# Audio tower: variance of a pair in two steps, a new order of all steps, and filling products behind the last round

## The chip, the cores and the metric

The kernel runs on one core of a Trainium2 chip. The metric is the device time of one execution in microseconds; lower is better. A core has five engines that run their own queues in order and meet at semaphores: PE (TensorE, matrix products), DVE (VectorE), ACT (ScalarE), POOL (GpSimd) and SP (SyncE, which issues DMAs).

## What is computed

The input is 64 records of 4000 samples. A tower of seven convolutions without padding follows (128 channels; taps and strides 10/5, four times 3/2, twice 2/2), each with a layer norm over the channels and an exact GELU. It leaves 12 positions for each record, 768 tokens of 128 channels. Then come a layer norm, a projection to 192, a Nyström attention with 64 landmarks and a mixture of eight experts with two chosen, beside a shared expert. The change touches the tower alone:

```python
for w, g, b, s in zip(conv_ws, ln_gs, ln_bs, strides):
    h = _conv1d(h, w, s)
    h = jnp.swapaxes(h, -2, -1)
    h = _fp32_layernorm(h, g, b)
    h = jnp.swapaxes(h, -2, -1)
    h = jax.nn.gelu(h, approximate=False)
```

## The kernel before, in words

The records go through the tower in four rounds of 16. A round has two slots (s = 0, 1) of eight records. Layers 0 to 3 are done round by round. Layers 4 to 6 take all 64 records at the end, and there a slot is half of them: slot 0 of layer 4 holds rounds 0 and 1, slot 1 rounds 2 and 3, and its pair p is the round 2s + p.

The order of all work is one list of steps, written out by hand. ROUND_ORDER is played once for each turn; a step is named what.layer.slot.p, a "+" in front means that it belongs to the next round, a "-" to the round before. LAST_ORDER is played once behind the turns. tower_plan makes the list and numbers the steps. Each engine walks the whole list and issues only what is its own share of each step, with waits for the numbers that it needs. So the list sets the order on every engine at once, and a step whose input is late holds up all that stands behind it on that engine. The steps:

- prep (parts 0 to 13) and phases: the windows of layer 0 for the next round, made by VectorE (and one copy on GpSimd for phases), written to DRAM and read back by SP's DMAs.
- first: layer 0 of one record, two bf16 matmuls (L476); ScalarE does the GELU (L562).
- half, conv: a pair of chunks of 400 columns. In layers 1 to 3 (PAIRED) half issues the middle tap (L499) and a product shared by both chunks (L502, ScalarE copies it); GpSimd forms a difference for conv (L457), which adds the outer taps (L508). VectorE writes the pair to SBUF (L682, in layers 4 to 6 L685) and ScalarE squares it (L579). In layers 4 to 6 half and conv are the two chunks (L522).
- var: the sum over channels of the squares of a pair, by matmuls in which the squares are the weights and one column of constants streams (L536): eight fp32 matmuls, which the profile shows as 16 instructions, since each fp32 matmul is two passes.
- norm: VectorE turns the variances of a whole slot into three bf16 parts of 1/sqrt(v + eps), 15 small operations (L694 to L706).
- rows: PE transposes them (L546), VectorE copies (L709). scale: PE spreads the row over the partitions (L553), VectorE multiplies one chunk (L715). gelu: ScalarE, on two chunks (L584).

PE has two banks for pairs and firsts, two for scales, and one for the shared product. There are two buffers of squares: ScalarE's square of a pair waits until the variance of the pair two before is done.

Before the change, half.4.0.0 stands behind all steps of layer 3 of the last round. Behind the tower, the attention's own products begin.

## Time and profile before

| what | value |
|---|---|
| median of 3 runs | 904.41 us (904.39 to 908.73) |
| the profiled execution | 903.9 us |
| its span | 901.8 us |
| PE busy | 752.5 us (83%) |
| VectorE busy | 640.3 us (71%) |
| ScalarE busy | 331.3 us (37%) |
| GpSimd busy | 313.0 us (35%) |
| mean granted clock of TensorE | 0.92 of full |

The span begins with the windows of round 0 (to about 55 us); the rounds fill 55 to about 447 us, the last layers end at 520.3 us, and attention and experts fill the rest. A busy PE isn't a PE at full speed: the granted clock tells at which of its two levels (1.2 or 2.4 GHz) it ran. Busy time is that of instructions, and an instruction lasts longer at the lower clock.

### The profile page before, as it was taken

To read this page: it belongs to the slowest core of one execution; us is meant where nothing else is said; L and a number is where in the kernel's file an instruction comes from. 1 tells how busy PE (TensorE), PEld (TensorE's weight loads), DVE (VectorE), ACT (ScalarE), POOL (GpSimd) and SP (SyncE) were. 2 spreads that over 40 slices of the span, in tenths; PEclk is the share of its full clock that TensorE was granted. 3 is DMA by queue.
4 is the path that set the end of the run, shared out by engine and by line. 5 is a ranking of instruction groups with operands and counts; after the bars stand their busy time and mean duration, and the time that the engine had idled before them with its cause. 6 is when DMAs were issued, how large, how long until landed. Compare 5 with 4: busy or idle time off the path is not lost. (4 is left out here: it accounts for less than half of the span.)

```text
span 901.8 us, 11857 instructions
## 1 busy us (share of the span) xinstructions
PE 752.5 (83%) x4259; PEld 574.4 (64%) x4259; DVE 640.3 (71%) x1447; ACT 331.3 (37%) x562; POOL 313.0 (35%) x365
## 2 busy tenths in 40 slices
PE   0039999999999999999787578788888888899987
PEld 0016565565655665665554477768788887899977
DVE  3946867887788966546646566998888888553387
ACT  0034456354544564454313215113333231346333
POOL 3003320412231312222100006475788787238301
PEclk9999978999799988998989589989999999989999
DMA  1360150006100330000000070000000000200000
GB/s 60 45 133 1 35 115 1 1 1 124 26 1 1 62 76 0 1 1 1 1 0 1 1 323 2 1 1 1 1 1 1 2 1 1 80 1 1 1 1 26
DMA packets 22564, 25.48 MB, mean 28 GB/s; under 512 B 17052, under 2 KB 21212, under 8 KB 21404
## 3 DMA queue, kind: packets, MB, share of 16 engines
q1 hardware_dynamic: 22508, 24.74, 11.2%
q8 instruction: 34, 0.56, 0.3%
q14 instruction: 22, 0.18, 0.1%
HBM read 21.05 MB, written 3.66 MB: 27 GB/s over the span
## 5 line engine op out<-in xcount | busy, mean ns | idle before, releaser
L457 POOL TENSOR_TENSOR diff<-h 128x400 f32<-128x400 f32 x112 | 97.6, 895 | 300.0 <-ACT h L562 135.1
L536 PEld LDWEIGHTS ps<-averager,sq 128*100 128x100 f32 (+2 forms) x1024 | 103.2, 176 | 16.7 <-ACT sq L579 8.1
L499 PE MATMUL ps<-h,w 128*128 128x400 f32 x224 | 109.9, 620 | 1.3 <-ACT h L584 0.5
L536 PE MATMUL ps<-averager,sq 128*100 128x1 f32 (+2 forms) x1024 | 101.1, 229 | 4.0 <-ACT sq L579 3.9
L682 DVE TENSOR_TENSOR h<-ps,shared 128x800 f32<-128x800 f32 x56 | 55.4, 989 | 57.2 <-PE ps L508 53.8
L579 ACT ACTIVATE sq<-h 128x800 f32<-128x800 f32 (+1 forms) x58 | 50.1, 864 | 118.7 <-DVE h L682 112.6
L508 PE MATMUL ps<-diff,w 128*128 128x400 f32 x224 | 91.1, 528 | 0.0
L1023 PE MATMUL pt<-for_pe,ident 128*128 128x156 f32 (+2 forms) x420 | 67.0, 318 | 23.4 <-DVE for_pe L1222 23.4
L562 ACT ACTIVATE h<-ps,lnp 128x800 f32<-128x800 f32 x64 | 63.5, 1014 | 47.5 <-PE ps L476 47.1
L1023 PEld LDWEIGHTS pt<-for_pe,ident 128*128 128x128 f32 x420 | 60.7, 196 | 28.5 <-DVE for_pe L1222 26.1
L476 PE MATMUL ps<-late,w_stack 90*128 90x400 bf16 x128 | 35.9, 383 | 49.1 <-DMA late<-windows_dram 45.0
L715 DVE TENSOR_TENSOR h<-h,ps 128x400 f32<-128x400 f32 (+1 forms) x116 | 61.0, 559 | 18.8 <-PE ps L553 17.7
L584 ACT ACTIVATE h<-h,lnp 128x800 f32<-128x800 f32 (+1 forms) x58 | 59.8, 1045 | 37.9 <-DVE h L715 36.7
L980 PE MATMUL pt<-ident 128*128 128x128 f32 x542 | 69.5, 289 | 0.0
L499 PEld LDWEIGHTS ps<-h,w 128*128 128x128 f32 x224 | 46.3, 219 | 35.3 <-issue 32.6
L980 PEld LDWEIGHTS pt<-ident 128*128 128x128 f32 x542 | 67.7, 205 | 0.6 <-issue 0.4
L508 PEld LDWEIGHTS ps<-diff,w 128*128 128x128 f32 x224 | 42.7, 198 | 28.9 <-issue 26.7
L476 PEld LDWEIGHTS ps<-late,w_stack 90*128 90x128 bf16 x128 | 12.5, 113 | 70.0 <-issue 57.8
L1242 DVE TENSOR_REDUCE e<-from_pool 128x54 f32<-128x702 f32 (+8 forms) x117 | 56.7, 550 | 0.3
L502 PE MATMUL ps<-h,w_sum 128*128 128x400 f32 x112 | 56.6, 590 | 0.0
L1023 PE MATMUL pt<-pool_for_pe,ident 128*128 128x132 f32 (+3 forms) x420 | 56.5, 292 | 0.0
L1088 POOL TENSOR_TENSOR from_pool<-e,c 128x702 f32<-128x702 f32 (+8 forms) x54 | 50.2, 973 | 18.0 <-DVE c L1324 18.0
(283 smaller groups left out, 1369.4 us busy)
## 6 DMA issues: line engine op xcount, KB each, us to landing
late<-windows_dram SPq DMA_DIRECT2D x24, 375.0 KB, 7.6
gate_w<-in_gate_w SPq DMA_DIRECT2D x1, 3456.0 KB, 14.0
up_w<-in_up_w SPq DMA_DIRECT2D x1, 3456.0 KB, 19.3
windows_dram<-parts SPq DMA_DIRECT2D x12, 250.0 KB, 5.4
acts<-in_down_w SPq DMA_DIRECT2D x1, 1728.0 KB, 8.1
w<-in_w SPq DMA_DIRECT2D x1, 1024.0 KB, 5.3
xs<-in_x SPq DMA_DIRECT2D x4, 252.5 KB, 4.7
out_tokens<-hidden SPq DMA_DIRECT2D x6, 96.0 KB, 1.6
```

What stands on the lines that cost most here:

```text
L457: pool.tensor_tensor(to[:, rows, :], here[:, rows, :], behind[:, rows, :], ALU.subtract).then_inc(diff_ready, 1)
L499: pe.matmul(out[:, c, :, :], w[:, L.first_tap + 1, :], plane(l, s, p, 1, slice(c, L.pos, 2)), start=True, stop=False)
L502: pe.matmul(shared_ps[:, 0:L.cols].rearrange("p (b t) -> p b t", t=L.pos // 2), w_sum[:, l - 1, :], plane(l, s, p, 0, slice(1, L.pos, 2)), ...
L508: mm = pe.matmul(out[:, c, :, :], w[:, L.first_tap + 2 * c, :], diffs(l, n["paired"] % RING, slice(c, L.pos, 2)), start=False, stop=True)
L536: mm = pe.matmul(var_ps[0:L.w, at:at + 1], sq[:, square_of[r, l, s, p] % 2, c, q * L.w:(q + 1) * L.w], averager[:, 0:1], start=True, stop= ...
L562: act.activation(h0[:, s, p, :, 0:POS0 // 2], ypair[b][:, :, 0:400], ACT.Gelu, scale=lnp[:, 0:1], bias=lnp[:, 1:2]).then_inc(y_taken, 1)
L584: act.activation(both, both, ACT.Gelu, scale=lnp[:, 2 * l:2 * l + 1], bias=lnp[:, 2 * l + 1:2 * l + 2]).then_inc(gelu_done, 1)
L682: nc.vector.tensor_tensor(to, src, both.unsqueeze(1).broadcast_to([P, 2, 2 * L.per_chunk, L.pos // 2]), ALU.add).then_inc(y_copied, 1)
L715: nc.vector.tensor_tensor(h, h, spread[n["scale"] % 2][:, 0:L.cols].rearrange("p (b t) -> p b t", t=h.shape[2]), ALU.mult).then_inc(scaled, 1)
L980: pe.matmul(to[:, 0:P], ident[:, :], ident[:, :], start=True, stop=True)
L1023: mm = pe.matmul(job.banks(n)[:, 0:wide], ident[:, :], sum_buffers[n][:, k * wide:(k + 1) * wide], start=(k == 0), stop=(k == job.terms - 1))
L1242: nc.vector.tensor_reduce(job.out(i), pooled_row(job, i), AX.X, ALU.add).then_inc(row_done, 1)
```

## The change

- A var step now covers one chunk of a pair instead of two (p counts chunks): eight passes instead of 16, each step with its own increment of var_done. ScalarE's square waits for both steps of the pair two before.
- ROUND_ORDER is new throughout. conv.1.0.0 of the next round now closes a turn. The four scales and two gelus of layer 3 stand further back in the next turn, behind steps of layers 1 and 2.
- There are turns only up to the last but one; LAST_ORDER now holds the whole last round, with layer 4's slot 0 between the steps of layer 3, and the last layers in a new order. The wait of layer 4's half and conv asks for the gelus of the one round that they read.
- A new step fill.0.0.n issues n products of 400 bf16 columns (ident16 by pick) into the bank of the shared product. Nothing reads them. LAST_ORDER has 13 such steps with 46 products.

```diff
--- before.py
+++ after.py
@@ -123,27 +123,41 @@
 
 
 ROUND_ORDER = """
-    conv.1.0.0 half.1.0.1 prep.0.0.4 first.0.0.5 -var.3.1.0 -norm.3.1.0 conv.1.0.1 var.1.0.0 -scale.3.0.0 prep.0.0.5 half.1.0.2
-    first.0.1.0 prep.0.0.6 conv.1.0.2 prep.0.0.7 prep.0.0.8 var.1.0.1 -rows.3.1.0 half.1.0.3 prep.0.0.9 first.0.1.3 conv.1.0.3
-    var.1.0.2 prep.0.0.10 first.0.1.6 first.0.1.2 -scale.3.0.1 -gelu.3.0.0 var.1.0.3 half.1.1.0 norm.1.0.0 conv.1.1.0 half.1.1.1
-    rows.1.0.0 -scale.3.1.1 -scale.3.1.0 -gelu.3.1.0 conv.1.1.1 scale.1.0.2 var.1.1.0 prep.0.0.11 first.0.1.5 first.0.1.4
-    scale.1.0.1 scale.1.0.0 gelu.1.0.0 var.1.1.1 first.0.1.7 half.1.1.2 prep.0.0.12 scale.1.0.3 gelu.1.0.1 conv.1.1.2 prep.0.0.13
-    half.1.1.3 conv.1.1.3 half.2.0.0 scale.1.0.7 scale.1.0.4 var.1.1.2 scale.1.0.6 gelu.1.0.3 scale.1.0.5 gelu.1.0.2 var.1.1.3
-    norm.1.1.0 conv.2.0.0 half.2.0.1 rows.1.1.0 conv.2.0.1 scale.1.1.0 scale.1.1.1 gelu.1.1.0 var.2.0.0 scale.1.1.3 scale.1.1.2
-    gelu.1.1.1 scale.1.1.5 scale.1.1.6 +first.0.0.3 +first.0.0.7 scale.1.1.4 gelu.1.1.2 scale.1.1.7 gelu.1.1.3 var.2.0.1 half.2.1.0
-    +phases.0.0.0 norm.2.0.0 +first.0.0.0 conv.2.1.0 rows.2.0.0 half.2.1.1 +prep.0.0.0 scale.2.0.0 +first.0.1.1 scale.2.0.1
-    gelu.2.0.0 conv.2.1.1 scale.2.0.3 scale.2.0.2 gelu.2.0.1 +first.0.0.6 +prep.0.0.1 var.2.1.0 var.2.1.1 half.3.0.0 norm.2.1.0
-    +first.0.0.4 conv.3.0.0 +first.0.0.1 rows.2.1.0 scale.2.1.3 scale.2.1.2 gelu.2.1.1 scale.2.1.1 scale.2.1.0 gelu.2.1.0
-    +prep.0.0.2 var.3.0.0 +first.0.0.2 half.3.1.0 norm.3.0.0 conv.3.1.0 +half.1.0.0 +prep.0.0.3 rows.3.0.0
+    -var.3.1.1 prep.0.0.3 -var.3.1.0 -norm.3.1.0 half.1.0.1 var.1.0.1 first.0.1.6 conv.1.0.1 prep.0.0.4 var.1.0.0 half.1.0.2
+    first.0.1.1 prep.0.0.5 prep.0.0.6 prep.0.0.7 conv.1.0.2 prep.0.0.8 prep.0.0.9 var.1.0.2 half.1.0.3 var.1.0.3 -rows.3.1.0
+    conv.1.0.3 var.1.0.4 var.1.0.5 first.0.1.4 first.0.1.5 var.1.0.6 var.1.0.7 prep.0.0.10 norm.1.0.0 first.0.1.3 half.1.1.0
+    -scale.3.1.0 first.0.1.7 conv.1.1.0 rows.1.0.0 prep.0.0.11 half.1.1.1 conv.1.1.1 prep.0.0.12 var.1.1.1 var.1.1.0 scale.1.0.3
+    half.1.1.2 scale.1.0.1 conv.1.1.2 var.1.1.3 var.1.1.2 half.1.1.3 prep.0.0.13 scale.1.0.2 gelu.1.0.1 var.1.1.4 scale.1.0.0
+    gelu.1.0.0 conv.1.1.3 var.1.1.5 scale.1.0.5 scale.1.0.7 half.2.0.0 scale.1.0.6 gelu.1.0.3 scale.1.0.4 gelu.1.0.2 conv.2.0.0
+    var.1.1.6 var.1.1.7 norm.1.1.0 half.2.0.1 conv.2.0.1 var.2.0.1 rows.1.1.0 -scale.3.0.1 scale.1.1.2 +first.0.0.4 +phases.0.0.0
+    +first.0.0.6 scale.1.1.5 var.2.0.3 scale.1.1.3 gelu.1.1.1 scale.1.1.1 var.2.0.0 scale.1.1.0 gelu.1.1.0 scale.1.1.4 gelu.1.1.2
+    +first.0.0.3 var.2.0.2 scale.1.1.7 scale.1.1.6 gelu.1.1.3 norm.2.0.0 half.2.1.0 conv.2.1.0 half.2.1.1 -scale.3.0.0 -gelu.3.0.0
+    rows.2.0.0 -scale.3.1.1 -gelu.3.1.0 conv.2.1.1 scale.2.0.0 scale.2.0.1 gelu.2.0.0 +first.0.0.1 var.2.1.0 scale.2.0.3 scale.2.0.2
+    gelu.2.0.1 var.2.1.3 +prep.0.0.0 var.2.1.1 var.2.1.2 +first.0.0.0 +first.0.1.0 +first.0.1.2 norm.2.1.0 half.3.0.0 rows.2.1.0
+    +first.0.0.2 scale.2.1.1 scale.2.1.0 gelu.2.1.0 conv.3.0.0 scale.2.1.2 scale.2.1.3 gelu.2.1.1 +prep.0.0.1 +first.0.0.5 var.3.0.0
+    var.3.0.1 norm.3.0.0 half.3.1.0 conv.3.1.0 +half.1.0.0 +prep.0.0.2 +first.0.0.7 rows.3.0.0 +conv.1.0.0
 """
 
 LAST_ORDER = """
-    half.4.0.0 conv.4.0.0 half.4.0.1 var.4.0.0 conv.4.0.1 half.4.1.0 var.4.0.1 norm.4.0.0 conv.4.1.0 half.4.1.1 rows.4.0.0
-    scale.4.0.0 scale.4.0.1 gelu.4.0.0 var.4.1.0 conv.4.1.1 scale.4.0.2 scale.4.0.3 gelu.4.0.1 half.5.0.0 var.4.1.1 norm.4.1.0
-    conv.5.0.0 rows.4.1.0 scale.4.1.0 scale.4.1.1 gelu.4.1.0 var.5.0.0 scale.4.1.2 scale.4.1.3 gelu.4.1.1 norm.5.0.0 half.5.1.0
-    rows.5.0.0 scale.5.0.0 scale.5.0.1 gelu.5.0.0 conv.5.1.0 half.6.0.0 var.5.1.0 norm.5.1.0 conv.6.0.0 rows.5.1.0 scale.5.1.0
-    scale.5.1.1 gelu.5.1.0 var.6.0.0 norm.6.0.0 half.6.1.0 rows.6.0.0 scale.6.0.0 scale.6.0.1 gelu.6.0.0 conv.6.1.0 var.6.1.0
-    norm.6.1.0 rows.6.1.0 scale.6.1.0 scale.6.1.1 gelu.6.1.0
+    -var.3.1.1 -var.3.1.0 -norm.3.1.0 half.1.0.1 var.1.0.1 first.0.1.6 conv.1.0.1 var.1.0.0 half.1.0.2 first.0.1.1 conv.1.0.2
+    var.1.0.2 half.1.0.3 var.1.0.3 -rows.3.1.0 conv.1.0.3 var.1.0.4 var.1.0.5 first.0.1.4 first.0.1.5 var.1.0.6 var.1.0.7 norm.1.0.0
+    first.0.1.3 half.1.1.0 -scale.3.1.0 first.0.1.7 conv.1.1.0 rows.1.0.0 half.1.1.1 conv.1.1.1 var.1.1.1 var.1.1.0 scale.1.0.3
+    half.1.1.2 scale.1.0.1 conv.1.1.2 var.1.1.3 var.1.1.2 half.1.1.3 scale.1.0.2 gelu.1.0.1 var.1.1.4 scale.1.0.0 gelu.1.0.0
+    conv.1.1.3 var.1.1.5 scale.1.0.5 scale.1.0.7 half.2.0.0 scale.1.0.6 gelu.1.0.3 scale.1.0.4 gelu.1.0.2 conv.2.0.0 var.1.1.6
+    var.1.1.7 norm.1.1.0 half.2.0.1 conv.2.0.1 var.2.0.1 rows.1.1.0 -scale.3.0.1 scale.1.1.2 scale.1.1.5 var.2.0.3 scale.1.1.3
+    gelu.1.1.1 scale.1.1.1 var.2.0.0 scale.1.1.0 gelu.1.1.0 scale.1.1.4 gelu.1.1.2 var.2.0.2 scale.1.1.7 scale.1.1.6 gelu.1.1.3
+    norm.2.0.0 half.2.1.0 conv.2.1.0 half.2.1.1 -scale.3.0.0 -gelu.3.0.0 rows.2.0.0 -scale.3.1.1 -gelu.3.1.0 conv.2.1.1 scale.2.0.0
+    scale.2.0.1 gelu.2.0.0 var.2.1.0 scale.2.0.3 scale.2.0.2 gelu.2.0.1 var.2.1.3 var.2.1.1 var.2.1.2 norm.2.1.0 half.3.0.0
+    rows.2.1.0 scale.2.1.1 scale.2.1.0 gelu.2.1.0 conv.3.0.0 scale.2.1.2 scale.2.1.3 gelu.2.1.1 var.3.0.0 var.3.0.1 norm.3.0.0
+    half.3.1.0 conv.3.1.0 rows.3.0.0 half.4.0.0 var.3.1.1 var.3.1.0 norm.3.1.0 conv.4.0.0 half.4.0.1 rows.3.1.0 conv.4.0.1
+    scale.3.1.0 scale.3.0.1 var.4.0.0 half.4.1.0 var.4.0.1 scale.3.0.0 gelu.3.0.0 scale.3.1.1 gelu.3.1.0 var.4.0.3 var.4.0.2
+    norm.4.0.0 conv.4.1.0 half.4.1.1 rows.4.0.0 fill.0.0.2 scale.4.0.1 scale.4.0.0 gelu.4.0.0 conv.4.1.1 var.4.1.0 half.5.0.0
+    var.4.1.2 scale.4.0.2 var.4.1.3 scale.4.0.3 gelu.4.0.1 var.4.1.1 norm.4.1.0 fill.0.0.4 conv.5.0.0 fill.0.0.3 rows.4.1.0
+    fill.0.0.2 scale.4.1.0 scale.4.1.1 gelu.4.1.0 var.5.0.1 scale.4.1.2 scale.4.1.3 gelu.4.1.1 var.5.0.0 half.5.1.0 norm.5.0.0
+    conv.5.1.0 fill.0.0.1 rows.5.0.0 fill.0.0.3 scale.5.0.1 scale.5.0.0 gelu.5.0.0 var.5.1.1 var.5.1.0 fill.0.0.3 half.6.0.0
+    norm.5.1.0 fill.0.0.1 rows.5.1.0 fill.0.0.2 scale.5.1.1 scale.5.1.0 gelu.5.1.0 conv.6.0.0 fill.0.0.2 half.6.1.0 conv.6.1.0
+    var.6.0.0 var.6.0.1 norm.6.0.0 fill.0.0.5 var.6.1.1 var.6.1.0 norm.6.1.0 fill.0.0.7 rows.6.0.0 fill.0.0.11 rows.6.1.0
+    scale.6.0.0 scale.6.1.0 scale.6.1.1 gelu.6.1.0 scale.6.0.1 gelu.6.0.0
 """
 
 
@@ -157,7 +171,7 @@
 def tower_plan():
 
     order = []
-    for turn in range(-1, ROUNDS + 1):
+    for turn in range(-1, ROUNDS - 1):
         for what, later, l, s, p in steps_of(ROUND_ORDER):
             r = turn + later
             if what in ("prep", "phases"):
@@ -165,15 +179,15 @@
                     order.append((what, r + 1, l, s, p))
             elif 0 <= r < ROUNDS:
                 order.append((what, r, l, s, p))
-    for what, _, l, s, p in steps_of(LAST_ORDER):
-        order.append((what, ROUNDS - 1, l, s, p))
+    for what, later, l, s, p in steps_of(LAST_ORDER):
+        order.append((what, ROUNDS - 1 + later, l, s, p))
     return counted(order)
 
 
 def counted(order):
 
 
-    n = dict.fromkeys(("pair", "half", "conv", "var", "norm", "rows", "scale", "gelu", "first", "prep", "phases", "paired"), 0)
+    n = dict.fromkeys(("pair", "half", "conv", "var", "norm", "rows", "scale", "gelu", "first", "prep", "phases", "paired", "fill"), 0)
     out, bank, held = [], 0, None
     users = [None, None]
     for what, r, l, s, p in order:
@@ -512,8 +526,7 @@
                         c = int(what == "conv")
 
                         if l == 4:
-                            newest = r if (s, p) == (1, 1) else r - 1
-                            pe.wait_ge(gelu_done, gelus_before(plan, newest, 3, 1)[0] + 1)
+                            pe.wait_ge(gelu_done, max(gelus_before(plan, 2 * s + p, 3, slot)[0] for slot in range(2)) + 1)
                         else:
                             done = gelus_before(plan, r, l - 1, s)
                             pe.wait_ge(gelu_done, done[min(2 * p + c, max(done))] + 1)
@@ -523,19 +536,23 @@
                                            start=(t == 0), stop=(t == L.taps - 1))
                         if c:
                             mm.then_inc(y_ready, 1)
+                    elif what == "fill":
+                        pe.wait_ge(shared_taken, n["paired"])
+                        for _ in range(p):
+                            pe.matmul(shared_ps[:, 0:400], ident16[0:96, :], pick[:, :, :].rearrange("p c n -> p (c n)")[:, 0:400],
+                                      start=True, stop=True)
                     elif what == "var":
 
-                        pe.wait_ge(y_taken, number_of(plan, "conv", r, l, s, p, "pair") + 1)
+                        pe.wait_ge(y_taken, number_of(plan, "conv", r, l, s, p // 2, "pair") + 1)
                         if n["norm"]:
                             pe.wait_ge(var_read, n["norm"])
                         if n["rows"]:
                             pe.wait_ge(rows_ready, n["rows"])
-                        for c in range(2):
-                            for q in range(4):
-                                at = var_at(l, s, q * L.chunks + 2 * p + c)
-                                mm = pe.matmul(var_ps[0:L.w, at:at + 1],
-                                               sq[:, square_of[r, l, s, p] % 2, c, q * L.w:(q + 1) * L.w], averager[:, 0:1],
-                                               start=True, stop=True)
+                        for q in range(4):
+                            at = var_at(l, s, q * L.chunks + p)
+                            mm = pe.matmul(var_ps[0:L.w, at:at + 1],
+                                           sq[:, square_of[r, l, s, p // 2] % 2, p % 2, q * L.w:(q + 1) * L.w], averager[:, 0:1],
+                                           start=True, stop=True)
                         mm.then_inc(var_done, 1)
                     elif what == "rows":
                         pe.wait_ge(rstd_ready, number_of(plan, "norm", r, l, s, 0, "norm") + 1)
@@ -575,7 +592,8 @@
                     elif what == "conv":
                         act.wait_ge(y_copied, n["conv"] + 1)
                         if n["conv"] >= 2:
-                            act.wait_ge(var_done, number_of(plan, "var", *conv_at[n["conv"] - 2], "var") + 1)
+                            r2, l2, s2, p2 = conv_at[n["conv"] - 2]
+                            act.wait_ge(var_done, max(number_of(plan, "var", r2, l2, s2, 2 * p2 + c, "var") for c in range(2)) + 1)
                         act.activation(in_banks(l, sq[:, square_of[r, l, s, p] % 2, :, 0:L.cols]), joined(l, s, p, r),
                                        ACT.Square).then_inc(y_taken, 1)
                     elif what == "gelu":
```

## Rows read from the trace of the kernel before

**Rows 1.** The page: granted TensorE clock in 40 slices, in tenths

```profile
PEclk9999978999799988998989589989999999989999
```

**Rows 2.** Busy time by stretch, us (x instructions); clock, DMA share, GB/s

```profile
165.40:261.00 95.60, 91.30 (x444) 57.12 (x443) 78.55 (x212) 47.48 (x58) 25.62 (x29) 0.89 0.18 36
69.80:446.90 377.10, 358.85 (x1746) 224.38 (x1745) 277.83 (x721) 181.96 (x221) 96.43 (x110) 0.90 0.13 27
356.60:446.90 90.30, 84.57 (x430) 53.68 (x429) 52.36 (x137) 39.87 (x50) 20.09 (x24) 0.92 0.00 1
446.90:479.30 32.40, 27.00 (x133) 16.75 (x131) 13.23 (x43) 6.68 (x7) 0.00 (x0) 0.89 0.00 1
479.30:520.30 41.00, 26.31 (x146) 17.23 (x144) 23.86 (x99) 10.23 (x12) 0.00 (x0) 0.70 0.00 0
```

**Rows 3.** Timeline of PE, round 2 to 3: start, duration, instructions

```profile
335.68 3.03 PE L536 MATMUL ps<-averager,sq 128*100 128x1 f32 x32
...
375.65 1.49 PE L536 MATMUL ps<-averager,sq 128*100 128x1 f32 x16
377.00 0.87 PE L476 MATMUL ps<-late,w_stack 90*128 90x400 bf16 x4
377.71 0.33 PE L553 MATMUL ps<-rows,pick 96*128 96x400 bf16 x1
```

**Rows 4.** Busy time by engine behind the variances at 335.68 us

```profile
338.80:342.20 3.40, 3.40 (x6) 1.53 (x6) 2.95 (x14) 0.33 (x1) 1.17 (x2) 0.52 0.00 0
```

**Rows 5.** Timeline of PE at full clock, layers one and two of the last round

```profile
398.61 1.56 PE L508 MATMUL ps<-diff,w 128*128 128x400 f32 x4
400.02 1.59 PE L499 MATMUL ps<-h,w 128*128 128x400 f32 x4
...
402.15 0.50 PE L553 MATMUL ps<-rows,pick 96*128 96x400 bf16 x2
402.50 1.49 PE L536 MATMUL ps<-averager,sq 128*100 128x1 f32 x16
```

**Rows 6.** Timeline of VectorE: first and last of the 15 operations of norm.6.1.0

```profile
514.73 0.16 DVE L694 TENSOR_SCALAR vs<-ps 48x8 f32<-48x8 f32 x1 [2.09 <-PE ps L536]
...
517.43 0.16 DVE L706 TENSOR_TENSOR rparts<-rest,rparts 48x8 bf16<-48x8 f32 x1
```

**Rows 7.** Timeline: one operation of prep.0; end of prep.13; next first

```profile
236.76 1.35 DVE L619 TENSOR_SCALAR u<-phases,gram 128x100 f32<-128x100 f32 x7
...
305.13 1.74 DVE L650 TENSOR_TENSOR parts<-u,parts 128x1000 bf16<-128x1000 f32 x1
...
320.84 0.87 PE L476 MATMUL ps<-late,w_stack 90*128 90x400 bf16 x4
```

**Rows 8.** Waits of PE in 69.8 to 446.9 us: total, times, longest

```profile
PE ps L553 <- DVE h L715: 5.8, 20, 0.6
...
PE ps L476 <- DMA late<-windows_dram: 1.1, 1, 1.1
```

**Rows 9.** Timeline of PE behind conv.3.1.0

```profile
448.93 1.57 PE L536 MATMUL ps<-averager,sq 128*100 128x1 f32 x16 [1.81 <-ACT sq L579]
...
453.58 0.57 PE L546 MATMUL ps<-ident,rparts 100*96 100x100 bf16 x4 [2.89 <-DVE rparts L706]
...
455.52 2.21 PE L522 MATMUL ps<-h,w 128*128 128x400 f32 x3
```

**Rows 10.** The page, costliest groups: busy, mean ns of one, idle before

```profile
L682 DVE TENSOR_TENSOR h<-ps,shared 128x800 f32<-128x800 f32 x56 | 55.4, 989 | 57.2 <-PE ps L508 53.8
L579 ACT ACTIVATE sq<-h 128x800 f32<-128x800 f32 (+1 forms) x58 | 50.1, 864 | 118.7 <-DVE h L682 112.6
...
L715 DVE TENSOR_TENSOR h<-h,ps 128x400 f32<-128x400 f32 (+1 forms) x116 | 61.0, 559 | 18.8 <-PE ps L553 17.7
L584 ACT ACTIVATE h<-h,lnp 128x800 f32<-128x800 f32 (+1 forms) x58 | 59.8, 1045 | 37.9 <-DVE h L715 36.7
```

**Rows 11.** Waits of PE in 446.9 to 520.3 us

```profile
PE ps L546 <- DVE rparts L706: 10.8, 6, 3.0
```

## The prediction, made before the changed kernel was run

> **What bounds the kernel now.** I read the strip of slices first: TensorE (PE) is near full from 55 us on, but its granted clock keeps dropping below full [rows 1]. Then the table of stretches, cut at the conv.1.0.0 of each round and at the end of layer three [rows 2]. A round of the tower lasts 95.6 us, with VectorE busy 78.55 us in it; the last round, which prepares no windows, needs 90.3 us to the end of conv.3.1.0 with VectorE at 52.36. So VectorE's load doesn't set the round; PE does, busy 91.3 and 84.6 us. The mean clock of 0.90 over the four rounds says that some 75 us of these 377 ran at 1.2 GHz instead of 2.4 (twice what is missing to 1.00). After layer three the picture changes: from 446.9 to 520.3 us PE is busy 53.3 of 73.4 us, at 0.89 and 0.70.
>
> What precedes a fall? The reader is to see PE's own instructions [rows 3]: at 335.68 us 32 one-column passes of variance run back to back (3.03 us, two pairs), at 375.65 one variance, two firsts, a scale, and a variance again. Behind the first the clock reads 0.52 in the following 3.4 us, with PE busy for all 3.40 [rows 4]. The 14 falls within rounds all followed two variances close together, or one beside scales that waited for VectorE. Not each such place fell: around 402.50 us stand a variance, two scales and a variance, and the clock stays full [rows 5].
>
> **The prices at full clock**, from start to start [rows 3, 5]: a conv 400.02 - 398.61 = 1.41 us, a half 402.15 - 400.02 = 2.13, a scale (402.50 - 402.15) / 2 = 0.17, a variance of a pair 377.00 - 375.65 = 1.35, a first (377.71 - 377.00) / 2 = 0.35. A round has 14 halves, 14 convs, 14 pair variances, 16 firsts, 28 scales and 6 rows (0.18, as a scale): 29.8 + 19.7 + 18.9 + 5.6 + 4.8 + 1.1 = 80 us. Three rounds of 80 and one of 75 up to the end of conv.3.1.0 (the eight firsts of a next round and what follows left out) make 315 us; the trace needs 446.9 - 69.8 = 377.1. Of these 62 us, 18 are PE idle [rows 2], and 75 us at half clock cost about 36: with every pass nearly twice as long they do the work of 39 (an estimate, by two clocks that stand 2 to 1). Some 8 stay unexplained.
>
> **The change part by part.**
> *Variance in two steps.* Same 16 passes, now 8 and 8. Nothing of PE's work goes; each round gets 14 more semaphore increments and waits. No stretch of the trace shows a cost of a step boundary on PE; between nothing and one pass (1.35 / 16 = 0.08) each, so 0 to 1.2 us a round; I take 0, as scale and variance follow each other without a gap [rows 3]. ScalarE's square of two pairs later now waits for both steps; in the new order both always come before that conv's copy, so this is covered.
>
> *New order in a round.* The sum of 80 stays. What can change is clock and idle. I added the prices along the new order to see where variances still cluster. The places of before had 2.7 us of variance together twice or more. In the new order most come as 0.7 us between halves and convs, or 1.4 us followed by a half. Three clusters are left: four steps of slot 0's layer one around first.0.1.4 and .5 (2.7 us in 3.4, just like the fall at 375.65); the ten scales of layer one's slot 1 with four steps and three firsts among them; and var.2.1.0, .3, .1, .2 within 5 us. I take half of the clock's cost as gone: -18 us over the rounds, from 0 (they fall as before) to -36.
>
> Idle: three chains come closer. (1) prep.10 stands before norm.1.0.0 on VectorE and rows.1.0.0 only 4.5 us of PE work behind the last variance; a norm takes 517.43 + 0.16 - 514.73 = 2.9 us [rows 6], 3.2 with wider tiles (an estimate from it); a wait of about 0.5. (2) prep.0 (ten operations, seven of which take 1.35 us, so 1.9 in all [rows 7]) now stands before norm.2.1.0, and rows.2.1.0 only 2.1 us of PE work (half.3.0.0) behind: copy, four scales, prep.0 and the norm reach it about 1.6 us late; behind it on PE are scales of layer two, conv.3.0.0 and half.3.1.0, so the round gets it whole. The last round has no prep. (3) The windows: prep.13 ends at 306.87 and the first of the next round runs at 320.84 [rows 7], 14.0 us later, and the windows come barely in time (in one round PE waited 1.1 us for them [rows 8]). By prices 11.6 us of PE work lie between the two in the new order and 11.2 before, and before the stretch lost 2.8 us to clock and waits, which the new one may not. So 0 to 2 us of new wait a round. SP's issues themselves stay the same 9 a round; the phases copy on GpSimd moves ahead of the diff of half.2.1.0 and is hidden, GpSimd being busy 26 us of 95.6 [rows 2]. Against that the old scales' waits for VectorE (5.8 us over the rounds [rows 8]) partly go, as they are spread between other work. Three rounds of 0.5 + 1.6 + 1 less some 3 of these: net idle +6 (from -6 to +15).
> Rounds together: -12, from -35 to +15.
>
> *Layer four among the last round.* Before, half.4.0.0 starts at 455.52, 8.6 us behind conv.3.1.0, because it stands in the queue behind rows.3.1.0 and its scales; in between PE waits 1.81 and 2.89 us for the square and the norm [rows 9]. Its inputs, rounds 0 and 1, were long done. Now half.4.0.0, conv.4.0.0, half.4.0.1 and conv.4.0.1 (about 2.06 us each) lie in those waits. I walked the new order from the end of conv.3.1.0 (T0, 446.9 before) with the copy 0.99, square 0.86, scale 0.56, gelu 1.05 [rows 10] and the norm of 3.2: norm.3.1 ready at T0+7.0, conv.4.0.1 done 10.0, gelu.3.1.0 16.8, conv.4.1.1 done 22.8. Before, conv.4.1.1 is done at 479.3, T0+32.4. After it: gelu.4.1.0 at 34.6, gelu.5.0.0 41.5, gelu.5.1.0 47.6, conv.6.1.0 done 49.5, norm.6.0 to 54.0 and norm.6.1 behind it to 57.0 (VectorE takes them one after the other now, since both variances come last), last gelu T0+60.5. Before: 73.4. So 13 us at full clock throughout.
>
> *Filling products.* 46 bf16 passes of 400 columns, 0.18 us each as a first's two passes of 400: 8 us. Each lies where PE waited for a norm or a gelu (10.8 us for norms alone behind layer three [rows 11]); the eleven before rows.6.1.0 end at T0+56.4, 0.6 us before norm.6.1. What they may buy is the clock (0.70 before). If the clock stays at half they take 0.33 each and the last group ends 2 us late. I take 10 of the 13, range 4 to 14.
>
> **Sum.** The profiled execution took 903.9 (span 901.8, 2.1 around it); the median is 0.5 above. 903.9 - 12 - 10 = 881.9; on the median 882.4, so 882. Attention and experts behind 520.3 move along unchanged; a warm clock at the hand-over may give up to 1 us, not counted.
>
> A rule of the Trainium skill speaks against the larger term ("TensorE: Matmul & The Clock Gate", "HAM oscillation — how this bites in real kernels"): the clock drops when PE sits idle between bursts of matmuls. By it variance passes, which keep PE issuing, would do no harm, and to place them apart would bring nothing. The trace disagrees so far: the fall after 335.68 us came with PE busy throughout [rows 3, 4].
>
> **The rivals.** Within 0.5% either way (4.5 us) a measurement here can't tell a change from none.
> A, forecast (chance 0.50): clock cost halved, tail shorter: 882, own range 865 to 893.
> B (0.19), the falls aren't made by the variances but by idle, or only move: rounds as before, only the tail gains: 904.4 - 10 = 894. For it: the two variances at 402.50 made no fall [rows 5]. Against: falls at full busy.
> C (0.12), falls all but vanish in the rounds and idle doesn't grow: 904.4 - 36 - 13 = 855.
> D (0.11), slower: prep.0 before norm.2.1.0 holds up layer two to three so far that each of the three preparing rounds loses more than the clock gives. It decides from 101 us a round on: 3 x 5.4 = 16, less the tail's 10: 910. For it: VectorE, busy 78.55 of 95.6 us, has little left if rounds get shorter. Against: the wait I find is 1.6.
> E (0.08), no change: rounds lose 8 to 12, as much as the tail gains: 904.
>
> Faster by over 0.5% (under 899.9): A, B, C = 0.81. Slower: D, 0.11. Same: 0.08. The range reaches from C to the edge of B: 854 to 900 leaves out D and E.
>
> **What would show it.** A round of 89 to 94 us instead of 95.6 with a mean clock of 0.94 or more; PE waiting 1 to 3 us for rparts ahead of rows.2.1.0; from the end of conv.3.1.0 to the last gelu 60 to 69 us, the first product on late at once behind it; a clock over 0.85 in layers five and six. Wrong if the clock in the rounds stays at 0.89 to 0.92 (B), or if waits for rparts or for windows exceed 8 us a round (D).

## The result and the profile after

The changed kernel takes 901.03 us (median of 20 executions, 892.38 to 905.92), the kernel before 905.71 beside it (20, 902.46 to 909.93). The ratio is 0.9947 with a 95% interval of 0.9928 to 0.9965: faster by 0.5%, about 4.7 us, where 22 were forecast. Ratios and intervals, here and below, leave out the executions in the slower of two states that the chip shows (one of these 20, and one of e5's six below), the medians don't. The profiled execution has a span of 898.8 us. First the page's strip of granted clock, which answers to [rows 1]; in slices 11 to 20 of the 40, within the rounds, 7999889989 has become 7899779988, and the 5 of the last layers a 6.

```profile
PEclk9999978989789977998898689987999999999999
```

The table of stretches answers to [rows 2]: four rounds, from conv.1.0.0 to conv.1.0.0, all four together, then from the end of conv.3.1.0 (T0 = 451.2) to the end of conv.4.1.1 and on to the last gelu.

```profile
70.50:166.30 95.80, 91.35 (x426) 55.98 (x424) 74.61 (x187) 45.78 (x56) 24.70 (x29) 0.88 0.18 36
166.30:265.90 99.60, 95.10 (x452) 59.48 (x450) 80.75 (x214) 48.26 (x59) 24.66 (x29) 0.86 0.17 34
265.90:363.50 97.60, 91.77 (x452) 57.05 (x450) 74.79 (x192) 49.13 (x60) 23.52 (x28) 0.90 0.16 32
363.50:451.20 87.70, 83.91 (x423) 54.12 (x420) 49.73 (x137) 38.96 (x48) 19.99 (x24) 0.90 0.00 1
70.50:451.20 380.70, 362.12 (x1739) 226.63 (x1737) 279.88 (x728) 182.13 (x220) 92.87 (x110) 0.88 0.13 26
451.20:474.50 23.30, 23.09 (x120) 14.78 (x119) 13.14 (x44) 6.57 (x7) 0.00 (x0) 1.00 0.00 1
474.50:516.60 42.10, 37.72 (x207) 22.83 (x205) 24.21 (x99) 10.12 (x12) 0.00 (x0) 0.73 0.00 1
```

The reader is to see three things. The rounds got longer, 377.1 to 380.7 us. PE's idle time in them stayed (18.3 to 18.6 us), but the time at 1.2 GHz (twice what the clock lacks to 1.00, times the stretch, summed over the four rounds) rose from some 75 to some 88 us. In steps of 0.5 us the clock stands at its lower level in 16 separate stretches before, 4.7 us long on average, and in 14 now, 6.3 us on average: it didn't fall more often, it came back later. And behind T0 the time fell from 73.4 to 65.4 us: conv.4.1.1 ends at T0 + 23.3 instead of + 32.4 at full clock, while the rest ran at 0.73.

Where falls lie in a preparing round: the same table over three of them.

```profile
319.50:333.30 13.80, 12.76 (x53) 8.29 (x53) 9.56 (x26) 8.32 (x9) 3.37 (x4) 0.63 0.37 80
343.60:350.40 6.80, 6.11 (x15) 2.74 (x16) 3.42 (x13) 2.99 (x4) 1.32 (x2) 0.51 0.00 0
507.30:521.00 13.70, 11.77 (x49) 7.33 (x48) 7.18 (x42) 2.98 (x5) 0.00 (x0) 0.50 0.17 35
```

The first is layer one's ten scales with variances and firsts among them, the second what follows the three variance steps at 340.54, both clusters that the prediction had named; the third is the end of the last layers and the attention's first 4 us. PE's timeline around them and at rows.1.0.0 (start, duration, instructions, idle before):

```profile
293.83 0.38 PE L563 MATMUL ps<-ident,rparts 100*96 100x100 bf16 x4 [2.13 <-DVE rparts L724]
...
340.54 2.21 PE L553 MATMUL ps<-averager,sq 128*100 128x1 f32 x24
...
349.30 0.54 PE L563 MATMUL ps<-ident,rparts 100*96 100x100 bf16 x4
...
354.21 1.57 PE L553 MATMUL ps<-averager,sq 128*100 128x1 f32 x16 [1.30 <-ACT sq L597]
```

The wait for the norm came at rows.1.0.0 (2.13 us at 293.83) and not at rows.2.1.0 (349.30, none). PE's waits from 70.5 to 451.2 us, which answer to [rows 8] (total, times, longest):

```profile
PE ps L553 <- ACT sq L597: 5.6, 4, 1.7
PE ps L563 <- DVE rparts L724: 3.7, 3, 2.1
PE ps L570 <- DVE rows L727: 3.1, 5, 0.8
PE ps L570 <- DVE h L733: 2.5, 9, 0.7
...
PE ps L490 <- DMA late<-windows_dram: 0.6, 2, 0.4
```

The scales' waits for VectorE fell from 5.8 to 2.5 us, and variances wait 5.6 us for ScalarE's squares instead (0.3 us before). Behind conv.3.1.0 PE now has work at once, where [rows 9] show two waits:

```profile
451.63 2.27 PE L535 MATMUL ps<-h,w 128*128 128x400 f32 x6
453.74 1.49 PE L553 MATMUL ps<-averager,sq 128*100 128x1 f32 x16
455.10 4.33 PE L535 MATMUL ps<-h,w 128*128 128x400 f32 x12
459.26 0.34 PE L563 MATMUL ps<-ident,rparts 100*96 100x100 bf16 x4
```

PE's waits for norms from 451.2 to 516.6 us, 10.8 us in [rows 11], are one now:

```profile
PE ps L563 <- DVE rparts L724: 1.5, 1, 1.5
```

### The profile page after: what moved, and what is told of

Read it like the earlier page. It is cut to its first block and busy times, and to the rows that moved or that the text cites. A ratio compares the mean times of both kernels' runs of the same rounds, so it can differ in the third digit from the quotient of the medians.

```text
span 898.8 us, 12011 instructions
## 1 busy us (share of the span) xinstructions
PE 763.6 (85%) x4305; PEld 578.1 (64%) x4305; DVE 641.1 (71%) x1447; ACT 332.4 (37%) x562; POOL 309.1 (34%) x365
## 5 line engine op out<-in xcount | busy, mean ns | idle before, releaser
L471 POOL TENSOR_TENSOR diff<-h 128x400 f32<-128x400 f32 x112 | 94.1, 862 | 308.9 <-ACT h L602 184.7
L553 PEld LDWEIGHTS ps<-averager,sq 128*100 128x100 f32 (+2 forms) x1024 | 109.2, 178 | 31.6 <-issue 16.3
L553 PE MATMUL ps<-averager,sq 128*100 128x1 f32 (+2 forms) x1024 | 104.9, 229 | 5.8 <-ACT sq L597 5.6
L1041 PE MATMUL pt<-for_pe,ident 128*128 128x156 f32 (+2 forms) x420 | 68.7, 324 | 23.3 <-DVE for_pe L1240 23.3
L490 PE MATMUL ps<-late,w_stack 90*128 90x400 bf16 x128 | 39.1, 411 | 46.1 <-DMA late<-windows_dram 43.2
L591 ACT COPY shared<-ps 128x400 f32<-128x400 f32 x56 | 27.4, 489 | 81.4 <-PE ps L516 81.4
L639 DVE SCALAR_TENSOR_TENSOR u<-phases,gram,u 128x100 f32<-128x100 f32 x180 | 56.3, 377 | 0.8
```

Source lines behind the costliest of these rows:

```text
L471: pool.tensor_tensor(to[:, rows, :], here[:, rows, :], behind[:, rows, :], ALU.subtract).then_inc(diff_ready, 1)
L553: mm = pe.matmul(var_ps[0:L.w, at:at + 1], sq[:, square_of[r, l, s, p // 2] % 2, p % 2, q * L.w:(q + 1) * L.w], averager[:, 0:1], start=Tr ...
L639: steps.done(nc.vector.scalar_tensor_tensor(out=u[:, k, :], in0=tap(l), scalar=gram[:, k, l:l + 1], in1=u[:, k, :], op0=ALU.mult, op1=ALU. ...
L1041: mm = pe.matmul(job.banks(n)[:, 0:wide], ident[:, :], sum_buffers[n][:, k * wide:(k + 1) * wide], start=(k == 0), stop=(k == job.terms - 1))
```

## The experiments

All runs are cut alike: at the shared product of half.1.0.0 in each round, at that of half.3.1.0 in the last, and at the attention's first product. "Rounds" are the three preparing ones, "last" the fourth, "tail" the rest of the tower. Idle is the stretch less PE's busy time. Time at 1.2 GHz can be worked out as above, to some 3 us in the rounds, since the clock has two digits. The stretches are those of one profiled execution each, and some of these lie far from the median: e4's (896.52) is the fastest of its 12, e8's (919.60) the slowest of its 12, e5's (907.84) lies 6 us above its median. Every ratio is against the kernel before, run on the same chip; e1 to e4, e5 to e8, e9 to e12, e13 to e16 and e17 to e18 shared a chip each.

| kernel | median us | ratio, 95% interval | rounds: us, idle, clock | last: us, clock | tail: us, idle, clock |
|---|---|---|---|---|---|
| before | 905.71 | | 287.0, 12.5, 0.89 | 88.7, 0.92 | 76.0, 20.4, 0.79 |
| after | 901.03 | 0.9947 (0.9928 to 0.9965) | 293.8, 14.8, 0.88 | 86.7, 0.90 | 67.9, 4.9, 0.83 |
| e1 | 909.31 | 1.0014 (0.9995 to 1.0034) | 287.8, 12.5, 0.89 | 88.6, 0.92 | 76.0, 20.3, 0.79 |
| e2 | 900.57 | 0.9926 (0.9904 to 0.9949) | 288.7, 12.3, 0.89 | 88.6, 0.92 | 67.8, 4.9, 0.83 |
| e3 | 918.43 | 1.0107 (1.0069 to 1.0144) | 296.0, 14.2, 0.86 | 88.0, 0.89 | 82.5, 20.5, 0.71 |
| e4 | 905.66 | 0.9968 (0.9942 to 0.9994) | 293.9, 16.0, 0.88 | 85.5, 0.92 | 66.5, 13.3, 0.81 |
| e5 | 901.76 | 0.9906 (0.9871 to 0.9940) | 301.2, 21.3, 0.88 | 85.5, 0.92 | 67.9, 4.9, 0.83 |
| e6 | 910.17 | 1.0036 (1.0014 to 1.0059) | 297.1, 18.9, 0.89 | 89.9, 0.90 | 70.8, 4.8, 0.79 |
| e7 | 911.74 | 1.0021 (0.9991 to 1.0051) | 302.3, 18.8, 0.87 | 86.9, 0.91 | 68.8, 3.8, 0.80 |
| e8 | 912.86 | 1.0053 (1.0031 to 1.0075) | 304.1, 14.9, 0.87 | 91.6, 0.86 | 68.8, 3.8, 0.80 |
| e9 | 905.27 | 0.9964 (0.9942 to 0.9985) | 295.6, 16.4, 0.87 | 88.6, 0.89 | 64.9, 6.4, 0.84 |
| e10 | 902.42 | 0.9942 (0.9919 to 0.9965) | 297.1, 19.9, 0.89 | 88.6, 0.89 | 64.5, 6.9, 0.94 |
| e11 | 911.62 | 1.0029 (1.0009 to 1.0048) | 304.2, 16.9, 0.87 | 90.9, 0.89 | 64.9, 6.4, 0.84 |
| e12 | 897.60 | 0.9886 (0.9864 to 0.9907) | 287.3, 12.5, 0.89 | 88.7, 0.92 | 65.6, 8.0, 0.86 |
| e13 | 901.02 | 0.9943 (0.9908 to 0.9978) | 291.9, 15.0, 0.88 | 90.2, 0.88 | 68.8, 3.7, 0.80 |
| e14 | 893.47 | 0.9887 (0.9852 to 0.9923) | 295.2, 20.3, 0.90 | 85.5, 0.92 | 64.2, 7.1, 0.95 |
| e15 | 889.99 | 0.9830 (0.9796 to 0.9864) | 288.9, 9.2, 0.88 | 88.7, 0.92 | 64.1, 6.9, 0.94 |
| e16 | 887.76 | 0.9801 (0.9767 to 0.9835) | 285.1, 9.2, 0.90 | 88.0, 0.95 | 64.5, 6.6, 0.94 |
| e17 | 907.06 | 0.9969 (0.9946 to 0.9991) | 303.5, 18.7, 0.88 | 88.7, 0.91 | 64.4, 6.6, 0.94 |
| e18 | 893.44 | 0.9824 (0.9799 to 0.9849) | 287.9, 14.2, 0.90 | 88.6, 0.92 | 62.9, 4.7, 0.91 |

The stretches of the kernel before, then of the changed one; the fourth line is what follows the tower:

```profile
68.90:355.90 287.00, 274.48 (x1317) 170.92 (x1316) 225.47 (x584) 141.40 (x172) 76.15 (x87) 0.89 0.18 35
355.90:444.60 88.70, 82.97 (x424) 52.74 (x423) 51.66 (x133) 40.08 (x49) 20.68 (x25) 0.92 0.00 1
444.60:520.56 75.96, 55.60 (x283) 35.25 (x282) 37.80 (x147) 17.45 (x21) 0.00 (x0) 0.79 0.00 1
520.56:901.80 381.24, 328.66 (x2214) 311.61 (x2214) 285.49 (x463) 123.12 (x312) 203.99 (x231) 0.96 0.07 26
```

```profile
68.50:362.30 293.80, 279.01 (x1317) 172.80 (x1316) 230.15 (x591) 142.58 (x172) 72.31 (x86) 0.88 0.17 34
362.30:449.00 86.70, 82.91 (x421) 53.80 (x420) 47.90 (x126) 39.46 (x48) 20.56 (x25) 0.90 0.00 1
449.00:516.91 67.91, 63.01 (x329) 38.58 (x328) 39.18 (x154) 17.21 (x21) 0.00 (x0) 0.83 0.00 1
516.91:898.80 381.89, 327.08 (x2214) 308.89 (x2214) 285.62 (x463) 122.90 (x312) 203.72 (x231) 0.96 0.07 26
```

### Which part does what: e1 to e4

**e1**, the kernel before with each variance in two steps that stand next to each other:

```diff
-    ... conv.1.0.1 var.1.0.0 -scale.3.0.0 ...
+    ... conv.1.0.1 var.1.0.0 var.1.0.1 -scale.3.0.0 ...
```

> The order of before, with each variance cut into two steps that stand side by side, and no fills. Theory 1 (the rounds lost to the clock, because the new order puts variances in clusters): the cut itself costs nothing, so the time is that of before, 905 to 906.5. Rival (the 14 more increments and waits a round cost PE time): 4 rounds at about 1 us, 908 to 910.

The interval holds 1, and all stretches are within 1 us of before. The split alone costs nothing that can be measured.

**e2**, the old rounds and the new tail; **e3**, the new rounds and the old tail:

```diff
-    for turn in range(-1, ROUNDS + 1):
+    for turn in range(-1, ROUNDS):
...
-LAST_ORDER = """ half.4.0.0 conv.4.0.0 half.4.0.1 ...
+LAST_ORDER = """ half.4.0.0 var.3.1.1 var.3.1.0 norm.3.1.0 ... (the changed kernel's, behind rows.3.0.0)
```

> The rounds in the order of before (variance steps side by side), up to rows.3.0.0 of the last round; behind it the changed kernel's last layers with layer four among layer three, and its fills. Theory 1: the tail's 8 us are had without the loss of the rounds: 897 to 899. Rival (the gain of the tail hangs on the new last round, which is 2.4 us shorter in the profile): 901 or more.

> The rounds in the changed kernel's order, the last layers in the order of before behind all of layer three, without fills. Theory 1: the rounds cost 3.7 us in sum (6 in the three that prepare windows, less 2.4 in the last), so 909 to 911 (before plus 3.7). Rival (the rounds cost nothing and the tail gives nothing, the difference is spread elsewhere): 901 to 906.

The table of stretches for e2's rounds and tail, then for e3's:

```profile
70.20:358.90 288.70, 276.42 (x1318) 171.64 (x1317) 225.47 (x584) 141.63 (x172) 75.80 (x87) 0.89 0.18 35
447.50:515.33 67.83, 62.98 (x329) 38.83 (x328) 38.05 (x147) 17.22 (x21) 0.00 (x0) 0.83 0.00 1
```

```profile
68.90:364.90 296.00, 281.79 (x1318) 174.61 (x1317) 229.91 (x591) 142.25 (x172) 72.35 (x86) 0.86 0.18 34
452.90:535.39 82.49, 61.95 (x284) 40.09 (x282) 38.43 (x151) 17.32 (x21) 0.00 (x0) 0.71 0.00 0
```

The tail gives its 8 us behind the old rounds too. The new rounds alone make the kernel slower by 1.1%: their rounds cost 9 us in the profile, and behind them even the old tail is 6.5 us longer at the same idle time, with PE busy 62.0 instead of 55.6 us for as many instructions. That part is clock. Against the 3.7 us that were expected for the rounds, e3 lost 1.1% or some 10 us. The same comes out with other tails made later on: e12 against e9 is 897.60 / 905.27, 0.8% less with the old rounds, e15 against e14 889.99 / 893.47, 0.4% less. Between e2 and the changed kernel, and between e15 and e14, the intervals overlap; e3's lies clear of 1, and e12's clear of e9's. So one half of the change gained and the other lost some of it.

The profiles put together show more than one pair of them. The old order of the rounds stands in six kernels (before, e1, e2, e12, e15, e18), the changed one in eight (after, e3, e4, e5, e9, e10, e13, e14). Three rounds took 287.0 to 288.9 us in the six and 291.9 to 301.2 in the eight, 7.7 us more on average. Of this PE's busy time gives 2.6 (275.7 to 278.4 on average) and its idle time 5.0 (12.2 to 17.2). In e14 the new rounds ran at 0.90, PE was busy 274.9 us as before the change, and they still took 8.2 us more. So the new order loses more by waits than by the clock.

**e4**, the changed kernel without the fill steps (`fill.0.0.2`, `fill.0.0.4`, ... taken out of LAST_ORDER):

> The changed kernel without its 46 filling products. Theory 1 says that they hold the clock little, since it stood at 0.73 in layers five and six with them: 900 to 902, no change. Rival (they carry part of the tail's gain by way of the clock): 903 to 906.

In the profile the tail is shorter without them (66.5 against 67.9 us) though PE idles 13.3 instead of 4.9 us, and the clock is hardly lower (0.81 and 0.83). But this execution is 9 us below e4's median, and the median of 905.66 lies in the range of the rival (903 to 906), on a chip on which the kernel before took 907.44 instead of 905.71. The interval of e4 overlaps with the changed kernel's (0.9928 to 0.9965) and not with that of e5, the same kernel on another chip (0.9871 to 0.9940). Whether the fills as made bought nothing or some 0.2 to 0.6% isn't shown.

### The rounds: e5 to e8

**e5** is the changed kernel again, **e6** takes the named clusters apart, **e7** lets both norms pass the windows' preparation, **e8** puts eleven fill products in each round:

```diff
-    ... half.2.1.1 -scale.3.0.0 ... conv.2.1.1 scale.2.0.0 ... var.2.1.0 scale.2.0.3 ... var.2.1.3 +prep.0.0.0 var.2.1.1 var.2.1.2
+    ... half.2.1.1 var.2.1.0 -scale.3.0.0 ... conv.2.1.1 var.2.1.1 scale.2.0.0 ... scale.2.0.3 ... var.2.1.3 +prep.0.0.0 var.2.1.2
...
-    ... prep.0.0.10 norm.1.0.0 ... +prep.0.0.0 var.2.1.1 var.2.1.2 ... norm.2.1.0
+    ... norm.1.0.0 prep.0.0.10 ... var.2.1.1 var.2.1.2 ... norm.2.1.0 +prep.0.0.0
...
-    ... var.2.0.3 scale.1.1.3 ... scale.1.1.1 var.2.0.0 scale.1.1.0 ... var.2.0.2 scale.1.1.7
+    ... var.2.0.3 fill.0.0.1 scale.1.1.3 fill.0.0.1 ... scale.1.1.1 fill.0.0.1 var.2.0.0 fill.0.0.1 scale.1.1.0 ... var.2.0.2 fill.0.0.2 scale.1.1.7
```

(e6 also moves var.1.0.4 and var.2.0.0 ahead of a conv; e8 has five more products around var.2.1.0 to .2 and before var.3.0.0.)

> The changed kernel itself, as the mark for the runs beside it. Theory 1 and its rivals alike: 0.9947 of before, within the interval of the first measurement (0.9928 to 0.9965); rounds that prepare windows 293 to 296 us together in the profile, the last 86 to 88, the tail 68.

> The changed kernel with five variance steps moved ahead: one of slot 0's layer one in front of conv.1.0.3, var.2.0.0 in front of conv.2.0.1, var.2.1.0 behind half.2.1.1 and var.2.1.1 behind conv.2.1.1, so that the clusters among scales and firsts lose half of their variances. Theory 1 (clusters of one-column passes make the clock fall, and that is what the new rounds lose): time at half clock in the three preparing rounds falls from 70 us to 45 or less, and these rounds from 294 to 284 or less; 892 to 896 in all. Rival (the falls come from PE's idle, or are bound to other work): half-clock time stays at 60 to 75 us and the time within 2 us of the changed kernel.

> The changed kernel with prep.10 behind norm.1.0.0 and prep.0 behind norm.2.1.0 on VectorE. The rival that VectorE's queue costs the rounds expects the 2.1 us wait before rows.1.0.0 to go in each preparing round and some more at rows.2.1.0: 4 to 7 us less than the changed kernel. Theory 1 expects 0 to 2 us, since PE's idle time in these rounds is only 2.3 us more than before the change (14.8 against 12.5).

> The changed kernel with ten more filling products a round, between the variances and scales of layers one and two and before var.3.0: 1.8 us of added work on PE in each round, some of it in waits. Theory 1 (what counts is how much PE streams; wide products beside the variances keep the clock up): half-clock time in the preparing rounds falls by 15 us or more, and the time is 2 to 6 us below the changed kernel although work is added. Rival (the order alone matters): half-clock time unchanged and 4 to 7 us slower.

e5 shows how loose the new order is. In another execution the same kernel took 7.4 us more in its rounds, 6.5 of them as idle, where 293 to 296 us in all were expected. PE's waits in e5's rounds, of which the changed kernel had none of the first, as much of the second and 0.6 us of the third:

```profile
PE ps L490 <- DVE h L700: 4.2, 2, 2.1
PE ps L553 <- ACT sq L597: 3.9, 3, 1.3
...
PE ps L490 <- DMA late<-windows_dram: 2.8, 3, 1.1
```

The 20 executions of the changed kernel spread over 13.5 us, the 20 of the kernel before beside it over 7.5.

e6 lost 0.9% against e5 (910.17 / 901.76), where 892 to 896 us or the changed kernel's own time were expected. Time at 1.2 GHz in the rounds went from 70 to 72 us only to 65, not to 45, idle stood at 18.9, and in the last round nothing was won. Its variances, now close behind their convs, wait for squares more often. The waits of e6's rounds, then of e7's:

```profile
PE ps L554 <- ACT sq L598: 5.9, 6, 1.3
```

```profile
PE ps L553 <- ACT sq L597: 7.7, 6, 1.8
...
PE ps L563 <- DVE rparts L724: 1.3, 2, 0.8
```

e7 cut the wait for the norm from 3.7 to 1.3 us and got 3.8 more of waiting for squares; it took 1.1% more than e5, which neither of its two expectations had. e8 was to hold the clock and didn't: 0.87 in the rounds and 0.86 in the last, 91.6 us, and slower by more than even its rival allowed. None of the three edits turned the loss. As each moved other waits too, they show that it isn't cured at one of these places, not that the place has no part in it.

### What a filling product must be: e9 to e14

e4 and e8 raised the question why products on a PE that would else wait don't keep its clock. The edits of the one matmul, each at the same places of the tail:

```diff
-  for _ in range(p): pe.matmul(shared_ps[:, 0:400], ident16[0:96, :], pick[...][:, 0:400], ...)
+e9:   for _ in range((p + 2) // 3): pe.matmul(shared_ps[:, 0:P], ident[:, :], ident[:, :], ...)
+e10:  for _ in range(p): pe.matmul(shared_ps[:, 0:400], ident16[:, :], parts[:, 0, 0:4, :] as 400 columns, ...)
+e13:  for _ in range(p): pe.matmul(shared_ps[:, 0:400], ident16[0:96, :], parts[0:96, 0, 0:4, :] as 400 columns, ...)
+e14:  for _ in range(p): pe.matmul(shared_ps[:, 0:384], ident16[:, :], ident16[:, :] three times, ...)
```

All but e9 issue 46 products; e9 20. e11 is e9 with six fp32 products a round as well, near e8's places; e12 is e9's tail behind the old rounds.

> The changed kernel with its fills as fp32 products of 128 columns (ident by ident, the attention's own warm products), one for each three or part of three bf16 ones: 20 instead of 46, about 9.8 us of PE instead of 8.2. New theory 2 (bf16 products, the fills, firsts and scales, count little for the clock; fp32 products do): the tail from half.3.1.0 to the attention shortens from 67.9 us to 62 to 65 and its half-clock time from 23 us to 10 or less. Rival (the clock follows how many columns stream, in which the new fills are the poorer): half-clock time 23 us or more and the tail 68 to 71.

> The changed kernel with its 46 fills still bf16 and of 400 columns, but with all 128 rows and with the windows of the last round as data in place of 96 rows of zeros and ones. Theory 2 (the kind of product counts): tail and half-clock time as in the changed kernel, 67.9 and 23 us. Rival (rows or data count): half-clock time 15 us or less.

> The changed kernel with all fills fp32 as in e9, and six such products a round in layers one and two and ahead of var.3.0, where e8 had ten bf16 ones: 2.9 us of work a round. Theory 2: the long fall among the scales of layer one shortens from 10.2 to 13.7 us to 7 or less, half-clock time of the three preparing rounds falls from 70 to 79 us to 50, and the time is 6 to 15 us below that of e8. Rival: as e8, 1.005 of before.

> The kernel of e2 (rounds in the order of before, new last layers) with the fp32 fills of e9. Theory 2: e2's 0.9926 of before less another 3 us, 0.989. Rival: 0.9926 or slower.

e9 kept the tail at 0.84, e10 at 0.94. So e10, of the same type as the changed kernel's fills, owes its clock to something else that it had changed, its data (the windows' bf16 parts, dense, where pick is mostly zeros) or its rows (128 for 96). e13 and e14 part the two.

> The changed kernel with its 46 fills on 96 rows as they are, but streaming the windows of the last round instead of zeros and ones. Theory 3a (dense data holds the clock): tail 64 to 65 us with 8 us or less at half clock, as e10. Theory 3b (the number of rows does): 67.9 and 23 us, as the changed kernel. Both in part: between.

> The changed kernel with fills of 128 rows that stream three times the identity (384 columns, one 1 in each). Theory 3a (dense data): 67.9 us and 23 us at half clock, as the changed kernel. Theory 3b (rows): 64 to 65 us and 8 us or less.

The tails of e9, e10, e13 and e14, one fence each:

```profile
452.90:517.84 64.94, 58.57 (x323) 40.73 (x322) 38.34 (x149) 17.21 (x21) 0.00 (x0) 0.84 0.00 1
```

```profile
454.90:519.36 64.46, 57.57 (x329) 36.22 (x328) 38.16 (x148) 17.11 (x21) 0.00 (x0) 0.94 0.00 1
```

```profile
450.10:518.90 68.80, 65.08 (x329) 40.02 (x328) 38.55 (x150) 17.22 (x21) 0.00 (x0) 0.80 0.00 1
```

```profile
448.70:512.87 64.17, 57.02 (x330) 35.73 (x328) 39.03 (x154) 17.11 (x21) 0.00 (x0) 0.95 0.00 1
```

Dense data on 96 rows: 0.80. Almost nothing but zeros on 128 rows: 0.95. It is the rows. The other kernels agree: seven with the 96-row fills have a tail at 0.79 to 0.83 (after, e2, e5 to e8, e13), six with 128 rows one at 0.91 to 0.95 (e10, e14 to e18). The fills ahead of rows.6.0.0 and behind it in the changed kernel (this view ends at 512 us, with eight of the eleven), and both in e14:

```profile
506.90 2.17 PE L542 MATMUL ps<-pick,ident 96*128 96x400 bf16 x7
...
509.44 2.85 PE L542 MATMUL ps<-pick,ident 96*128 96x400 bf16 x8
```

```profile
505.24 1.31 PE L542 MATMUL ps<-ident 128*128 128x384 bf16 x7
...
506.96 1.96 PE L542 MATMUL ps<-ident 128*128 128x384 bf16 x11
```

The 96-row passes slow down in the middle of their own run, from the 0.18 us each of [rows 3]'s bf16 passes to some 0.35 (2.85 / 8), with no idle time ahead; the 128-row ones go through at 0.19 (1.31 / 7) and 0.18 (1.96 / 11). On one chip e14 is 0.8% faster than e13 (893.47 / 901.02; the medians differ, the intervals of the two overlap), and in the profiles its tail is 4.6 us shorter and what follows the tower 4.9.

Within the tail the clock is worth less than these 4.6 us suggest. e9's tail at 0.84 took 64.9 us, only 0.7 more than e14's at 0.95, and e4's without any fill 66.5 at 0.81. The 46 fills of the changed kernel take up to 0.35 us each where the clock is low, and PE is busy 63.0 of its 67.9 us, against 53.2 of 66.5 in e4. The higher clock at the end of the tail pays behind the tower. That stretch in e9, then in e14:

```profile
517.84:901.50 383.66, 331.73 (x2214) 314.09 (x2214) 285.80 (x463) 122.70 (x312) 203.86 (x231) 0.95 0.07 26
```

```profile
512.87:891.60 378.73, 324.46 (x2214) 306.75 (x2214) 285.88 (x463) 122.89 (x312) 203.90 (x231) 0.97 0.07 26
```

Two things stay open: why fp32 products on 128 rows did less (there were 20 of them for 46), and e11's rounds, slower than any before.

### The two put together: e15 to e18

**e15** is the old rounds with e10's tail. **e16** adds ten products a round of the same kind (128 rows; their second operand is half of the weights' bits, since the windows' tile is in use), **e17** gives the new rounds e8's eleven in the same form. **e18** is e15 with the scales' own products on 128 rows, the 32 new ones zero.

```diff
+e16:  ... scale.1.1.3 fill.0.0.1 scale.1.1.2 fill.0.0.1 gelu.1.1.1 scale.1.1.5 fill.0.0.1 scale.1.1.6 fill.0.0.1 ... var.2.1.1 fill.0.0.2 var.2.1.2
...
-e18:  rows = sb("rows", [96, SETS, 400], BF16)
+e18:  rows = sb("rows", [P, SETS, 400], BF16)     (pick alike; rows is set to zero once)
```

> Rounds in the order of before, new last layers, and the dense fills of 128 rows of e10. Under 3a and 3b alike the tail is that of e10 (64.5 us), so 3.3 us less than e2 (0.9926 of before): 0.989. Rival (e12's fp32 fills, 0.9886, gave as much, so clock isn't what the tail waits for): no better than 0.9886.

> As e15, with ten dense bf16 fills of 128 rows in each round: six among the ten scales of layer one's slot 1, two between the variances of layer two's slot 1, two among its last scales (1.8 us of PE work a round, partly in waits). Theory 3 (a or b; the rounds' falls are like the tail's): half-clock time in the three preparing rounds falls from 63 us to 45 or less, and the time is 3 to 8 us below e15. Rival (the rounds' falls come from the one-column passes, which fills beside them don't change): half-clock time 60 us or more and 3 to 6 us slower than e15.

> The kernel of e8 with its fills on 128 rows instead of 96, in rounds and tail. Theory 3b (rows fed count for the clock): half-clock time in the three preparing rounds 45 to 60 us instead of e8's 79, the tail 64.5 us, and at least 10 us faster than e8: 0.985 to 0.993 of before. Rival (the rounds' falls come from the variances' one column, whatever stands beside): 75 us or more at half clock, only the tail's 3.5 us gained: 1.000.

> The kernel of e15 with the scales' products on 128 rows (rows 96 to 127 are zeros in both operands); the number and length of instructions are the same. Theory 3b: less half-clock time in the rounds (69 us in e15's profile, 63 in e2's) by 10 us or more and the time 2 to 5 us below e15's 0.983. Rival (only what is added between matters): 0.981 to 0.985, half-clock time 63 to 70 us.

The rounds and the last round of e15, then of e16:

```profile
69.30:358.20 288.90, 279.69 (x1317) 174.35 (x1316) 226.80 (x584) 141.29 (x172) 75.63 (x87) 0.88 0.18 35
358.20:446.90 88.70, 82.96 (x424) 52.63 (x423) 51.59 (x133) 40.04 (x49) 20.62 (x25) 0.92 0.00 1
```

```profile
69.50:354.60 285.10, 275.93 (x1347) 172.43 (x1346) 225.09 (x584) 141.37 (x172) 75.37 (x87) 0.90 0.18 35
354.60:442.60 88.00, 82.81 (x434) 51.81 (x433) 51.34 (x132) 40.06 (x49) 20.64 (x25) 0.95 0.00 1
```

e15 came out faster than expected (0.983 for 0.989). e16 issues 40 more products (x1347 and x434) and PE is busy 3.8 us less in its rounds than in e15's, about as much as the other kernels with that order without fills (273.7 to 276.4). Its 285.1 us are 1.9 less than the shortest of the six kernels with the old order, and its last round runs at 0.95 where those all stand at 0.92. So the clock paid for the fills and a little more. It was to fall to 45 us at 1.2 GHz and bring 3 to 8 us; it came to 57 and brought 2.2. At 0.9801 it is the best version, 2.0% below the kernel before and 0.25% below e15 on its chip; the intervals of the two overlap, so the tail and the old rounds are the sure part. In the new rounds products of this kind didn't do it: e17's rounds took 303.5 us at 0.88, e8's 304.1 at 0.87, and its ratio of 0.9969 missed the 0.985 to 0.993 expected. From e8 to e17 the ratio falls by 0.8%, but in the profiles the rounds give 0.6 us of it, the tail and the last round 7.3 (68.8 to 64.4 and 91.6 to 88.7). e18 has less time at 1.2 GHz in the profiled rounds than e15 (58 against 69 us), but 5 us more idle, and the same ratio, within its rival's range (0.981 to 0.985).

## Why the prediction was wrong

- **"I take half of the clock's cost as gone: -18 us over the rounds."** This is the step that failed. Time at 1.2 GHz rose by some 13 us instead of halving; the three preparing rounds' PE was busy 279.0 us instead of 274.5 with the same instructions, and e5 shows 279.9. The reason behind it, that variance passes close together make the falls, was read from falls behind two variances; in steps of 0.5 us the four rounds before show 16 falls, not 14. The new order has fewer such clusters, and the falls became 14 but longer (6.3 us on average for 4.7). Taking more of the clusters apart (e6) brought back 5 to 7 us at 1.2 GHz and no time. Why the clock stays low longer in the new order isn't shown. What runs did show to move the clock is how many rows a filling bf16 product feeds (e13, e14), and that helped in the old rounds (e16) and not in the new (e17).
- **"Net idle +6 (from -6 to +15)."** By the stretches +0.3 in the execution compared, but +8.8 in the three rounds of e5, and +5.0 in three rounds on average over eight profiles. The range held; the terms within it didn't. The norm was late at rows.1.0.0 (2.13 us, and not 0.5), at rows.2.1.0 it was in time (1.6 forecast). PE's waits for squares came to 5.6 us, for which the sum had no term: the prediction had only asked whether a square waits for a variance (it doesn't, ScalarE shows no such wait), not whether a variance, now close behind its conv, waits for its square. Waits for windows were 0.6 in one execution and 2.8 in the other (0 to 2 a round forecast).
- **"Rounds together: -12."** They lost 3.6 us by the marks of [rows 2], inside -35 to +15 but on the other side of nothing. Alone (e3 against before), the new rounds make the kernel slower.
- **Layer four among the last round.** The walk held: conv.4.1.1 at T0 + 23.3 for 22.8, and layer four's first product began 0.4 us behind T0. It ends at T0 + 65.4 where the walk at full clock said 60.5, so 8.0 of 13 us were won (10 forecast, 4 to 14). With 128-row fills the tail ends some 61.5 us behind T0 in e14 and e16: the walk was right, and what it lacked were fills that run at the higher clock. The clock of 0.73 behind conv.4.1.1 missed the sign of over 0.85.
- **"A warm clock at the hand-over may give up to 1 us, not counted."** Attention and experts took 381.2 us before and 381.9 after; in all six kernels with 128-row bf16 fills (e10, e14 to e18) 378.6 to 379.2, in e2, e5, e9, e12 and e13 381 to 384. It is worth 2 to 5 us, but the change as made didn't get it (e4's fastest execution, without fills, did, at 379.3).
- **The split** at nothing was right (e1).
- **The range.** The terms' own bounds, +15 for the rounds and -4 for the tail, reach 915; 854 to 900 left out the upper part, to which D and E were given 0.19 together, and 901.03 lies 1 us into it.
- **The rivals.** The result lies between B (chance 0.19), where the falls only move and the tail alone gains, 894, and E (0.08), where the rounds lose as much as the tail gains, 904: the rounds lost, but less than the tail gave. B's other half, that PE's idle time makes the falls, doesn't fit the tails: the Trainium skill ("TensorE: Matmul & The Clock Gate", "HAM oscillation — how this bites in real kernels") has the clock drop at waits of several microseconds between bursts of matmuls. No wait of PE for another engine in the changed tail is longer than 1.5 us; it idles 4.9 us in all and runs at 0.83, e14's idles 7.1 and runs at 0.95. So the page's case isn't the one met here.
- Sum of the profiled execution: three rounds +6.8, last round -2.0, tail -8.1, behind it +0.6, ahead of them -0.4: 901.8 to 898.8.

**What stays open**: why the new rounds cost more at all. Shown are the parts, on average 2.6 us of slower instructions and 5.0 of waits in three rounds (4.5 and 2.3 in the execution compared), and that no single edit of the clusters (e6), the late norms (e7) or the fill (e8, e11, e17) turns it. No run puts back the places of the old order's steps one group at a time. Where falls start is not set by the order alone: the last round of the same kernel took 86.7 us at 0.90 and, in e5, 85.5 at 0.92.

## What to carry to other kernels

Price a new order by its waits and passes, and walk the waits of every engine for every other: the tail, walked so, came within 1 us in 23, while in the rounds the wait for squares was left out. But give a hoped-for rise of the clock no sum until one small experiment has moved it. Where a bf16 step only fills PE to hold its clock, try it on all 128 rows, look at the granted clock of the stretch with and without, and count what the next stage gains. And time the halves of a large change apart: here one half gave 0.7%, and the other lost 0.4% to 1.1% wherever it was measured apart from the change's own tail.

## What the hardware showed that I had not expected

- Fills of bf16 on 96 rows left the last layers at a clock of 0.79 to 0.83, whatever their data; on 128 rows they held 0.94 to 0.95, even with one-hot data (0.91 in e18, whose scales' products had changed too). PE was busy 63.0 to 66.0 us with the first and 57.0 to 58.2 with the second: a fuller PE had the lower clock.
- fp32 products on 128 rows, 20 instead of 46, came to 0.84 and 0.86.
- In the changed kernel the clock fell from 2.4 to 1.2 GHz in the midst of a run of 96-row filling products, at 507.3 us, and the profile shows no wait of PE from 499 to 512 us. From 503.9 us to the fall PE was busy throughout, with two variances of 16 passes and with fills:

```profile
503.90:507.30 3.40, 3.40 (x43) 2.45 (x43) 2.26 (x12) 0.52 (x1) 0.00 (x0) 1.00 0.00 0
```
